# Third and fifth adapter summed by TensorE, batch 2's bias beside the statistics of x1, six value parts ahead of the first step's output product

## What is computed

```python
def ffn(x, W, b, ids, weights):               # K = 8 adapters of 32
    out = einsum('k,kod,bsd->bso', weights, W[ids], x)
    return out + einsum('k,ko->o', weights, b[ids])

x = x + 0.5 * ffn(layernorm(x), ...)
x = x + attn(layernorm(x), ...)
x = x + 0.5 * ffn(layernorm(x), ...)

# attn:
h = layernorm(x); hh = time_shift(h)
xk, xv, xr = h * tm_k + hh * (1 - tm_k), ...   # k, v, r mixes
k, v, sr = xk @ Wk.T, xv @ Wv.T, sigmoid(xr @ Wr.T)
x = x + (sr * wkv(time_decay, time_first, k, v)) @ Wo.T      # wkv: a scan over 512 tokens
h = layernorm(x); hh = time_shift(h)
kk = square(relu(xk @ Wck.T))                  # 1024 hidden channels
return x + sigmoid(xr @ Wcr.T) * (kk @ Wcv.T)
```

## Time and profile before

| | |
|---|---|
| median of 3 runs | 429.35 us (428.96 to 429.48) |
| the profiled execution's own time | 429.45 us |
| its span in the trace | 427.3 us |
| PE busy | 414.7 us, 97% of the span |
| DVE busy | 372.0 us, 87% |
| ACT busy | 335.1 us, 78% |
| POOL busy | 180.2 us, 42% |
| transfers | 18.52 MB, mean 43 GB/s |

### The profile page before, as it was taken

The page is one execution under the profiler, slowest core; times in us unless marked ns, Lnnn a source line. Parts: engine busy times, 40 slices in busy tenths (PEclk is TensorE's granted clock), DMA queues, the critical chain, the costliest instruction groups (busy, mean ns, idle before and its releaser), DMA issues.

```text
span 427.3 us, 6400 instructions
## 1 busy us (share of the span) xinstructions
PE 414.7 (97%) x2074; PEld 336.2 (79%) x2074; DVE 372.0 (87%) x735; ACT 335.1 (78%) x680; POOL 180.2 (42%) x193
## 2 busy tenths in 40 slices
PE   8989989989999999999999999999999999999996
PEld 8865876668868887798769886888779876988895
DVE  2988989998879899998989898989999898979555
ACT  1157978998699969998799969996999479956830
POOL 1446052617173554627281827345461518043011
PEclk9999999999999999999999999999999999999999
DMA  6992010001000001000200020000000000000011
GB/s 195 379 398 89 2 49 0 2 1 52 0 0 2 25 28 48 0 26 1 76 0 3 23 74 2 0 26 25 3 0 25 2 25 0 3 24 27 0 51 50
DMA packets 15971, 18.52 MB, mean 43 GB/s; under 512 B 1082, under 2 KB 13634, under 8 KB 15938
## 3 DMA queue, kind: packets, MB, share of 16 engines
q1 hardware_dynamic: 14538, 17.05, 11.3%
q10 hardware_dynamic: 1400, 1.07, 0.9%
HBM read 13.92 MB, written 4.19 MB: 42 GB/s over the span
## 4 chain that ended last, share of the span: by engine, by line
PE 74%; DVE 2%; POOL 1%; issue 1%; ACT 0%; DVEq 0%; POOLq 0%
PE pair L492 20%; PE pair L370 10%; PE pair L382 10%; PE pair L466 6%; PE pair L467 6%; PE pair L470 6%; PE pair L360 6%; PE pair L351 4%; PE pair L436 1%; PE pair L440 1%; PE pair L437 1%; PE pair L513 1%; PE pair L512 1%; PE pair L516 1%; POOL xs L1463 1%
## 5 line engine op out<-in xcount | busy, mean ns | idle before, releaser
L492 PE MATMUL pair<-wcv_sb,kk 128*128 128x256 f32 x448 | 100.5, 379 | 0.6 <-ACT kk L757 0.6
L492 PEld LDWEIGHTS pair<-wcv_sb,kk 128*128 128x128 f32 x448 | 83.9, 190 | 12.0 <-ACT kk L757 1.2
L466 PE MATMUL pair<-xck_hi,wck_hi 128*128 128x512 f32 x128 | 54.8, 428 | 0.0
L470 PE MATMUL pair<-xck_lo,wck_hi 128*128 128x512 f32 x128 | 50.7, 396 | 0.0
L467 PE MATMUL pair<-xck_hi,wck_lo 128*128 128x512 f32 x128 | 50.6, 395 | 0.0
L753 ACT ACTIVATE kk<-pair 128x512 f32<-128x512 f32 x64 | 36.3, 590 | 14.2 <-PE pair L470 14.1
L1423 POOL TENSOR_TENSOR x2b<-xs,bias_bc 128x512 f32<-128x512 f32 (+1 forms) x16 | 20.4, 1276 | 55.0 <-DVE xcr L1133 32.2
L757 ACT ACTIVATE kk<-kk 128x512 f32<-128x512 f32 x64 | 36.4, 623 | 0.0
L1423 POOL TENSOR_TENSOR x<-x,bias_bc 128x512 f32<-128x512 f32 x14 | 18.0, 1290 | 42.4 <-DVE xcr_lo L1181 22.3
L1463 POOL TENSOR_TENSOR xs<-x,xa 128x512 f32<-128x512 f32 x16 | 20.4, 1276 | 33.7 <-DVE xa L1114 33.7
L1449 POOL TENSOR_TENSOR xr<-xr,h 128x512 f32<-128x512 f32 x16 | 18.7, 1191 | 28.4 <-ACT xr L813 28.4
(11 more groups left out here) (181 smaller groups left out, 1132.7 us busy)
## 6 DMA issues: line engine op xcount, KB each, us to landing
x<-in_x_dram SPq DMA_DIRECT2D x8, 512.0 KB, 4.1
out_dram<-xs SPq DMA_DIRECT2D x15, 256.0 KB, 2.1
xt<-in_xt_dram SPq DMA_DIRECT2D x4, 512.0 KB, 7.9
work<-in_ffn_w_dram ACTq DMA_DIRECT2D x4, 256.0 KB, 4.9
work<-in_ffn_w_dram SPq DMA_DIRECT2D x4, 256.0 KB, 5.1
kk<-in_wck_dram SPq DMA_DIRECT2D x1, 1024.0 KB, 9.7
xs<-in_xt_dram SPq DMA_DIRECT2D x2, 512.0 KB, 11.8
wcv_sb<-in_wcv_dram SPq DMA_DIRECT2D x1, 1024.0 KB, 13.4
```

The lines of the kernel that those rows point to most:

```text
L466: nc.tensor.matmul(key_bank(n), wck_hi[:, h, cols], xck_hi[:, h, :], start=h == 0, stop=False)
L470: last = nc.tensor.matmul(key_bank(n), wck_hi[:, h, cols], xck_lo[:, h, :], start=False, stop=h == CH - 1)
L492: last = nc.tensor.matmul(bank_of("kv", e, i)[:, t % TB * C:(t % TB + 1) * C], kk[:, n, tok:tok + P], wcv_sb[:, n, :], start=n == 0, stop= ...
```

## The change

Three things are changed.

First, the adapters with the numbers 2 and 4 (`ON_PE`) are no longer added by DVE. DVE makes four 128x128 matrices, the two centring matrices times the two gates, in the idle tile `normed`; PE multiplies them with the two adapters as these land, and adds the six others' centred sum into the same PSUM banks. `warm` goes from 40 matmuls to 16, the bias product comes behind the sum, and ACT copies `ffn_t` first and then the bias.

Second, the statistics of x of batch 1 move from DVE to ACT (`ON_ACT` from 2 to 1). POOL adds the bias to batch 1 before its inverse deviation is made, into `xs[2]`, and `add_first(1)` reads it there. POOL makes the inverse deviation and the bias of batch 2 ahead of `first_inverses(1)`, before the steps begin, where the bias had been in step 0.

Third, in step 0 six value parts stand ahead of the output product, and ACT makes the sixth square before `residual_of(1)`.

```diff
-    ON_ACT = 2
+    ON_ACT = 1
+    ON_PE = (2, 4)
+    X_OF_1 = 2
...
+        gated_centre = [[normed[:, 2 * k + i, 0:P] for i in range(2)] for k in range(len(ON_PE))]
...
             def ffn_setup():
                 pe.wait_ge(s_const, 4)
-                warm(3, 40)
+                warm(3, 16)
+                pe.wait_ge(s_gated_centre, 1)
+                for i, k in enumerate(ON_PE):
+                    pe.wait_ge(s_sel[k], 16)
+                    for a in range(CH):
+                        for h in range(CH):
+                            nc.tensor.matmul(pair[1][:, a, 0:C], gated_centre[i][a != h], sel[:, k, h, :], start=i == 0 and h == 0, stop=False)
+                pe.wait_ge(s_ffn_acc, K - len(ON_PE))
+                for a in range(CH):
+                    for h in range(CH):
+                        last = nc.tensor.matmul(pair[1][:, a, 0:C], (centre_own if a == h else centre_other)[:, :], ffn_sum[:, h, :],
+                                                start=False, stop=h == CH - 1)
+                last.then_inc(s_ffn_ps, 1)
                 pe.wait_ge(s_gate_rows, 1)
                 pe.wait_ge(s_bias_sel, 16 * K)
                 nc.tensor.matmul(pair[0][:, 0, 0:C], gate_rows[:, :], bias_sel[:, :], start=True, stop=True).then_inc(s_bias_ps, 1)
-                pe.wait_ge(s_ffn_acc, K)
...
-                warm(3, 2)
...
-                channel_values(e, 0, range(WITHIN + (e == 0)))
+                channel_values(e, 0, range(WITHIN + 2 * (e == 0)))
...
             def setup_first():
+                act.wait_ge(s_ffn_ps, 1)
+                nc.scalar.activation(ffn_t[:, :, :], pair[1][:, :, 0:C], ACT.Copy).then_inc(s_ffn, 1)
                 act.wait_ge(s_bias_ps, 1)
                 nc.scalar.activation(bias_bc[:, :], pair[0][:, 0, 0:C], ACT.Copy).then_inc(s_bias, 1)
...
             setup_first()
+            stats_x(1)
             setup_second()
...
-                    for n in range(3, HB // 2 + 1):
+                    for n in range(3, WITHIN + 2):
                         key_square(e, n)
                     residual_of(f)
...
             stats_x(0)
             bias_to_first()
-            stats_x(1)
+            pads()
             add_first(0, (0,))
...
             def bias_to_x(b, i):
+                if b == 1:
+                    pool.wait_ge(x_loaded[b], 16)
+                    add_bias(tok_bank(xs[X_OF_1], i), tok_bank(x1[b], i), TB, xb_done)
+                    return
...
             inverse_x(0)
-            inverse_x(1)
             pool.wait_ge(s_bias, 1)
             bias_to_x(1, 0)
             bias_to_x(1, 1)
+            inverse_x(1)
             first_inverses(0)
...
             inverse_std("xa", 0)
+            inverse_x(2)
+            bias_to_x(2, 0)
+            bias_to_x(2, 1)
             first_inverses(1)
-            inverse_x(2)
...
                 if has(f + 1):
-                    if e == 0:
-                        bias_to_x(f + 1, 0)
-                    pool.wait_ge(aa_done, 2 * f + 2)
-                    bias_to_x(f + 1, 1)
+                    if e > 0:
+                        pool.wait_ge(aa_done, 2 * f + 2)
+                        bias_to_x(f + 1, 1)
```

More of the change, by code:

```diff
@@ L390, in ffn_setup @@
                 nc.tensor.matmul(pair[0][:, 0, 0:C], gate_rows[:, :], bias_sel[:, :], start=True, stop=True).then_inc(s_bias_ps, 1)
-                pe.wait_ge(s_ffn_acc, K)
-                for a in range(CH):
-                    for h in range(CH):
-                        last = nc.tensor.matmul(pair[0][:, 1, a * C:(a + 1) * C], (centre_own if a == h else centre_other)[:, :], ffn_sum[:, h, :],
-                                                start=h == 0, stop=h == CH - 1)
-                last.then_inc(s_ffn_ps, 1)
-                warm(3, 2)
             def first_product(f):
@@ L769, in last_weight_high @@
                     last = nc.scalar.activation(wcv_hi[i][:, :, :], wcv_sb[:, i * HB // 2:(i + 1) * HB // 2, :], ACT.Copy)
-                last.then_inc(s_wcv_hi, 1)
+                last.then_inc(s_wcv, 1)
             def channel_gate(e):
@@ L910, in _ @@
                 if e == 0:
-                    for n in range(3, HB // 2 + 1):
+                    for n in range(3, WITHIN + 2):
                         key_square(e, n)
                     residual_of(f)
-                    for n in range(HB // 2 + 1, HB):
+                    for n in range(WITHIN + 2, HB):
                         key_square(e, n)
@@ L1009, in add_first @@
                     for t in range(i * TB, (i + 1) * TB):
-                        last = nc.vector.scalar_tensor_tensor(tile[:, t, :], product[:, t % TB, :], rstd_x[b % 2][:, t:t + 1], tile[:, t, :], ALU.mult, ALU.add,
+                        last = nc.vector.scalar_tensor_tensor(tile[:, t, :], product[:, t % TB, :], rstd_x[b % 2][:, t:t + 1], own[:, t, :], ALU.mult, ALU.add,
                                                               accum_out=sums["x1"][:, t:t + 1] if b >= SUMS_X1 else None)
```

45 lines of the change are left out of this document (28 added, 17 removed).

## The result

The changed kernel takes 427.44 us (median of 6 runs, 427.14 to 428.16), the kernel before beside it 429.42 us (6 runs, 428.96 to 430.18). The ratio is 0.9949, 95% interval 0.9933 to 0.9965. Six more runs on another chip gave 427.94 us against 429.67, ratio 0.9953, 0.9939 to 0.9967. Over all 12 the median is 427.74 us, some 1.9 us under before.

What follows compares the result with a forecast made beforehand. PE, busy 97% of the span, was taken as the bound, idling longest at the head. Gains 1.04 + 0.57 + 0 = 1.61 us from 429.45 give 427.84, the median 0.1 lower: 427.7 us, range 427.2 to 428.9.

Steps and rivals of the forecast that it cites:

- Part 1, the sum: Set-up: with adapters 2 and 4 on PE, adapter 6's landing limits DVE's sum, ending at 13.44, 0.75 us earlier.
- Part 2, DVE's list: Set-up: without batch 1's statistics on DVE the first product becomes the limit; first transposition at 24.3, gain 1.04 us.
- the cover: Set-up: POOL's constant and power end at 22.2, only 0.15 us before POOL must be free at 22.36.
- Part 3, POOL's bias: Step 0: moving batch 2's bias ends two DVE stalls, 0.42 us on the second scan and 0.15 on L1087; gain 0.57.
- So it costs nothing: Before the steps: batch 2's bias pair at its new place runs beside DVE's `bn_stats` and delays nothing.
- lost cover: Bias pair's new place: without `bn_stats` beside it, the pair would cost DVE one stall of about 0.4 us.
- Part 4: Step 0: the sixth value part fills PE's wait for `rwkv`, but its 0.43 us return as idleness; gain 0.
- Rival 1: Step 0: the scan stays slow, only L1087 returns 0.15 us; gain 1.19, 428.2 us; chance 0.17 alone.
- Rival 4: Step 0: PE bounds the second transposition, so the sixth part gains 0.43 us more; 427.3 us; chance 0.05.
- Rival 2: Set-up: POOL holds batch 0's normalisation, up to 0.75 us of the start lost; 428.5 us; chance 0.15 alone.
- Rival 3: Set-up: PE at its lower level, product starts at 20.7; 432.3 to 435.8, taken as 433 us; chance 0.07.
- the two gaps: Set-up: PE's idle gaps after the shorter warming, 1.3 and 0.7 us, expected to leave PE at its upper level.

Runs made afterwards that it cites:

- bias-in-step profile: Changed kernel with both halves of batch 2's bias put back in step 0; 428.19 us (8 runs), its profiled execution 427.76 us.
- its fill: Changed kernel with batch 1's statistics back on DVE and 6 warming matmuls ahead of the first transposition; 429.22 us (12 runs), ratio 0.9985.
- split bias: Changed kernel with the second half of batch 2's bias moved behind batch 1's inverse deviation and normalisation; 427.75 us (7 runs), its profiled execution 431.36 us.

## Why the prediction was right

The forecast was 427.7 us, and the 12 runs have their median at 427.74. Step by step:

**Part 1, the sum (0.75 us forecast at the product).** Right in mechanism: the adds end 1.61 us behind the landing of adapter 6. The size rests on one trace on either side. In the profiles of the kernels with two adapters on PE the last adds start anywhere from 11.27 to 12.26 and end from 12.88 to 13.87. With all eight on DVE the sum ended at 13.41, 13.90 and 14.19 in the three profiles there are, and the forecast compared with the last of them. In the profile of the changed kernel the gain at the product was 0.31 us. Undone, part 1 costs 0.5 us in the medians, some of which may belong to the 24 more warming matmuls that come back with it.

**Part 2, DVE's list (1.04 us carried on).** Right at the transposition. With the sum at its forecast place (13.44) PE's matmuls on it would start 0.06 us later, at 13.50, and the transposition 10.89 us behind them, at 24.4 against the 24.3 forecast. POOL's power of batch 0 took 1.04 us, as forecast, and that of batch 1 ended well ahead of `rboth`, which starts at 22.90: 21.24 + 1.03 = 22.27. So the cover was 0.6 us and not 0.15. The step that was off is the start of batch 0's statistics. The forecast had them wait for x until 13.87; in the bias-in-step profile they start at 13.11, right behind the sum, and there too the power ends (21.45) 0.6 us ahead of `rboth` (22.08). So POOL's work moves with the sum.

Most of the 1.04 us is the sum, which comes 0.75 us earlier in the forecast; from the sum's matmuls to the transposition the change gains 0.21 us (11.10 to 10.89). Undone in the changed kernel, part 2 costs 1.21 us, since the bias now comes 1.00 us later behind the sum. So the parts do not add up: undoing parts 1, 2 (with its fill) and 3 costs 0.5, 1.5 and 0.45 us by the medians, more than the 1.9 us of the whole. No run has the new list with the bias product ahead of the sum, so what that move costs or gives by itself is not known.

**Part 3, POOL's bias (0.57 us).** The gain is there in full in its terms, 0.44 for the scan and 0.15 for L1087. "So it costs nothing" is the step that was mis-sized: the forecast had DVE inside `bn_stats` while the pair runs, and overlooked the 128x4 instruction that follows it. That was held 0.84 us, nearly all that was left of POOL's pair (62.34 - 61.35 = 0.99, less 0.13 at the end), of which 0.2 us reached the transposition. The forecast's own figure for lost cover was 0.4 us. Net 0.42 us was measured, not 0.57.

**Part 4 (0).** Right, shown by its undoing.

**What was missing from the sum.** The time around the span fell from 2.16 us (median over the 73 runs of before that stood beside the experiments, 2.10 to 2.22) to 1.80 (12 runs, 1.74 to 1.86). It goes with part 2: with the statistics back on DVE it is 2.18 us (2.12 to 2.25), filled or not, while undoing part 1, 3 or 4 leaves it at 1.79 to 1.81. It is not part 2 alone: without warming matmuls and with one adapter on PE it is 1.90 and 1.89 us. So 0.36 us of the median's gain lies outside what the trace shows. The forecast used 2.15 us for both kernels. What it is, is not known. It made up for the 0.15 us too much in part 3 and for landings later than 11.8, so that the median came out within 0.05 us of the forecast is luck; the distances inside the traces, which bear out parts 2 to 4, are not. As a gain the forecast was 1.65 us and the measured one 1.9. With the 0.36 us the profiled executions add up: statistics on DVE starts its transposition 0.73 us later than the changed kernel, 0.73 + 0.36 = 1.09, and 429.26 less 428.16 is 1.10.

**Rival 1** (the scan stays slow) is out: the second scan takes 1.21 us. **Rival 4** (the sixth part pays) is out by its undoing. **Rival 2** (POOL holds the normalisation of batch 0) is out in both profiles of the changed kernel, and none of its 12 runs is long (428.16 us at most), but one execution of the split bias had it. **Rival 3** (PE at its lower level in the set-up) did not occur; the two gaps stayed at 1.19 and 0.73 us. The rise came inside the 16 warming matmuls, as forecast, but not always near 6.5 us: they took from 5.28 us (bias in step 0) to 6.73 us (statistics on DVE), so it comes earlier in some executions and later in others. The rival was closer than its chance of 0.07 said. Its reason, "no gap is longer than one already seen", held for the kernel as it is; one adapter fewer on PE and a milder form of it was there, in the sum's four matmuls alone, at 1.7 us a time.

The Trainium skill, in "TensorE: Matmul & The Clock Gate" (The HAM clock gate), says that the throttled state is the default and that activity lifts it. The run without warming agrees (5.96 us against 3.69), the run with one adapter shows the way back down (0.62 after 2.78 us idle).

## What to carry to other kernels

TensorE idling just before its critical work can pay twice, once for the wait and once at its lower clock. So before work is taken from TensorE's idle stretch or its gap is made longer, read the granted clock behind the gap, in several executions, and if it falls, fill the gap with useless matmuls: eight of them gave back 1.3 us. A fill has its own price: 40 warming matmuls at the start could hold the sum for 1.2 us when the level rose late. When an instruction of GpSimd is moved away from one that it holds up, look at every VectorE instruction beside the new place, the tiny ones too, since the stall is as long as what is left of GpSimd's instruction and not as long as its victim. And where a chain ends in a transfer's landing, take the landing's spread over several traces into the range. Last, undoing a part of a change prices it in the changed kernel, and not in the one it was made for; if the undoings add up to more than the whole, look for what the parts share.

## What the runs showed of the hardware

- VectorE and GpSimd hold each other, in both directions, up to about 0.13 us before the holder's end. GpSimd held a 128x4 TENSOR_SCALAR of DVE (0.17 us) for 0.84 us. DVE's L1290, 1.23 us from 17.00, held POOL's pair (3.54 us instead of 2.50), which gives a release at 18.09, 0.14 us before L1290's end. In the split-bias profile it held POOL's power in the same way (2.06 us instead of 1.04). Not every instruction is held: DVE's BATCH_NORM_STATS2 took its usual 1.40 us beside POOL's pair at 59.84. The Trainium skill, in "SBUF — State Buffer" (Who interferes with whom), also counts `tensor_scalar` in a two-port mode among the instructions that need the shared pair, and says that who issues first holds it; the 1.01 us agree with the first, and L1290 and L981 stand for the two orders.
- Idle times of PE of 1.04 to 1.24 us, and one of 2.25 us, left the granted clock at 1.00 behind them; 2.43 and 2.78 us were followed by stretches at 0.59 and 0.62. One execution of each was profiled, and the same kernels keep their clock in other executions.
- The granted clock's column read 1.00 over the 421 ns records at 4 to 6 us, which become 275 ns later in the same row of matmuls, so there the records' durations are what to read.
- The adds that wait for adapter 6 started at 11.27 us in one execution and at 12.26 in another, with the same loads issued in the same order.
- The time around the span changed by 0.36 us (2.16 to 1.80) with a change inside it, and came back (2.18) when part 2 was undone.
